# A decoder layer with a routed expert stage: a new order of work in the attention stage, and another way for the expert outputs, the token reads and the stores at the end

## The reference

```
x = x + attn(layernorm(x))            # causal sums of rank 128 (cumsum over tokens), 512 x 512 weights
x = x + xattn(layernorm(x), ctx)      # 16 heads of 32, softmax over the 750 context rows
x = x + ffn(layernorm(x))
# ffn: logits = x @ gate_w.T + gate_b;  probs = softmax over the tokens (axis -2)
#      each of 32 experts takes its 8 best tokens:  vals, idx = top_k(probs, 8)
#      merged[b, e] = sum_k vals * x[idx]                       (one row for each batch and expert)
#      o[b, e] = (gelu([merged, 1] @ w1[e]), 1) @ w2[e]          (513 x 2048, then 2049 x 512)
#      out[b, idx] += vals * o[b, e]                            (scatter back to the 8 tokens)
```

## Time and profile before

| | us |
|---|---|
| median of 3 runs | 2212.28 (2208.69 to 2214.53) |
| the profiled execution's own time | 2212.52 |
| its span | 2210.8 |
| PE busy, of 1290 us from 110 to 1400 us | 1256.5 |
| DMA rate from 1560 to 2100 us | 421 GB/s |

### The profile page before, as it was taken

How to read it: one execution, slowest core, us unless ns; L and a number is a source line. 1 busy time by engine, 2 the same in 40 slices (tenths; PEclk the granted TensorE clock), 3 DMA queues, 4 the chain that set the end, 5 groups by cost and what they waited for, 6 DMA issues and landing times. The chain is left out here.

```text
span 2210.8 us, 41404 instructions
## 1 busy us (share of the span) xinstructions
PE 1842.7 (83%) x12594; PEld 1207.2 (55%) x12594; DVE 1011.4 (46%) x2542; ACT 747.3 (34%) x1551; POOL 823.9 (37%) x591
## 2 busy tenths in 40 slices
PE   7889999999999999999999999986665656655644
PEld 5667777777777776777777767753111111111111
DVE  1355757657667676676676665751100000000003
ACT  3144435435454454454444544542100000000000
POOL 0255545555555556555555565552000000000000
PEclk9799999999999999999999999988877777777776
DMA  5324333243243333332433333266999999999996
GB/s 171 84 68 101 81 91 98 76 101 82 77 105 83 88 94 83 92 85 76 109 83 84 95 85 89 70 240 233 406 422 421 423 421 420 421 422 421 420 365 238
DMA packets 142370, 421.35 MB, mean 191 GB/s; under 512 B 32140, under 2 KB 78188, under 8 KB 117756
## 3 DMA queue, kind: packets, MB, share of 16 engines
q1 hardware_dynamic: 135580, 411.70, 54.6%
q10 hardware_dynamic: 5760, 8.15, 1.0%
q0 software_dynamic: 992, 1.02, 0.1%
HBM read 307.37 MB, written 17.14 MB: 147 GB/s over the span
## 5 line engine op out<-in xcount | busy, mean ns | idle before, releaser
L1172 DVE TENSOR_REDUCE maxes<-bank 112x1 f32<-112x376 f32 (+1 forms) x1024 | 511.3, 539 | 118.5 <-PE bank L1393 114.9
L974 ACT ACTIVATE probs<-bank 125x448 f32<-125x448 f32 x768 | 400.0, 547 | 140.5 <-PE bank L1415 139.5
L1809 PE MATMUL bank<-ring,hid_T 128*32 128x512 f32 x1024 | 177.9, 858 | 201.3 <-DMA ring<-in_L_ffn_w 196.4
L848 POOL TENSOR_TENSOR psum_keys<-psum_keys,probs 125x896 f32<-125x896 f32 x127 | 266.7, 2100 | 211.9 <-ACT probs L974 202.5
L1415 PE MATMUL bank<-q_st,k_st 98*125 98x224 f32 x1536 | 334.6, 304 | 8.5 <-DMA q_st<-max_two 5.6
L1393 PE MATMUL bank<-k_st,q_st 96*112 96x376 f32 (+1 forms) x1024 | 318.9, 357 | 21.3 <-DVE maxes L1172 18.1
L1415 PEld LDWEIGHTS bank<-q_st,k_st 98*125 98x125 f32 x1536 | 256.8, 190 | 61.3 <-issue 33.5
L1713 DVE TENSOR_TENSOR o_fin<-bank,b_row 16x512 f32<-16x512 f32 x32 | 21.7, 678 | 586.6 <-PE bank L1762 586.6
L851 POOL TENSOR_TENSOR psum_keys<-psum_keys,probs 125x896 f32<-125x896 f32 x127 | 266.8, 2100 | 10.0
L1642 POOL DMA_DIRECT2D o_rows<-o_fin x31 | 15.3, 492 | 595.4 <-DVE o_fin L1713 595.4
L1809 PEld LDWEIGHTS bank<-ring,hid_T 128*32 128x32 f32 x1024 | 44.9, 151 | 310.3 <-issue 304.8
(11 more groups left out here) (171 smaller groups left out, 2742.5 us busy)
## 6 DMA issues: line engine op xcount, KB each, us to landing
ring<-in_L_ffn_w SPq DMA_DIRECT2D x128, 2048.0 KB, 30.7
k_st<-k_hi SPq DMA_DIRECT2D x512, 93.8 KB, 2.1
k_st<-k_lo SPq DMA_DIRECT2D x256, 93.8 KB, 2.2
q_st<-q_hi SPq DMA_DIRECT2D x504, 28.0 KB, 1.8
ctx_nat<-in_ctx SPq DMA_DIRECT2D x16, 750.0 KB
x_in<-in_x SPq DMA_DIRECT2D x16, 448.0 KB, 3.9
out<-x SPq DMA_DIRECT2D x16, 448.0 KB, 3.1
out<-ring ACTq DMA_DIRECT2D x28, 256.0 KB, 3.1
```

The costliest lines, as they stand in the source:

```text
L848: nc.gpsimd.tensor_tensor(psum_keys[:], psum_keys[:], lo, ALU.add).then_inc(pool_chain, 1)
L974: nc.scalar.activation(probs[n % 2][:, j, :], bank[5 + u % 2][0:SK, 0:2 * T], ACT.Exp, scale=SCALE).then_inc(probs_ready, 1)
L1172: nc.vector.tensor_reduce(maxes[:, j, t, c:c + 1], score_bank(n)[0:TT, 0:SC[c + 1] - SC[c]], AX.X, ALU.max).then_inc(s_drained, 1)
L1809: last = nc.tensor.matmul(bank[5 + e2][c * 32:(c + 1) * 32, :], hid_T[:, e2, t, c * 32:(c + 1) * 32], ring[:, slot, col:col + D], start=(t ...
```

## The change

1. **A new table.** `TIMETABLE`, `AT`, `MAXIMA` and `SUM_AT` hold other steps, `LAST_PV_AT` is 2 instead of 1. The set of jobs and their sizes stay.
2. **Joined denominators.** `denominators` of a group is issued directly behind the `values` of its last third, instead of later in step 2.
3. **Expert outputs straight into the scatter's operand.** For experts 0 to 30 POOL issues four DMAs each, from `o_fin` into the rows of `o_in` (4 rows of 2 KB each). `o_rows`, the writes to it and the eight reads back are gone. DVE waits for these placements before it writes `o_fin` again.
4. **The last expert by TensorE.** A matmul with a 0/1 matrix `spread` (cleared by POOL, filled by one DVE copy) adds the four partial sums of the last expert and puts them into their rows in one step; DVE adds that to `o_in`, which holds b2 there (four small DMAs at the start of the stage). This is done once for each of the four quarters of `o_in`, the first ahead of the scatter, the others inside it. The last `sum_parts`, the last addition of b2 and the DMAs of L1630 are gone.
5. **The last w2 in another layout.** Its two chunks hold steps t = 0, 1 and t = 2, 3, so that PE starts the first half when the first chunk is there.
6. **The order of SP's queue.** All weights come first, and the token reads behind them. The last two experts are outside PE's loop.
7. **Stores on two queues.** ACT stores the tiles of even number in the order of work, SP those of odd number.

```diff
-LAST_PV_AT = 1
-SUM_AT = {5: 0, 11: 1, 14: 2}
+LAST_PV_AT = 2
+SUM_AT = {6: 0, 12: 1, 13: 2}
...
-MAXIMA = ((3, 3, 3, 1, 2, 2, 0, 0, 0, 1, 1),
-          (0, 1, 0, 0, 0, 3, 1, 3, 1, 2, 1, 2, 2),
-          (1, 2, 1, 0, 2, 2, 0, 2, 2, 0, 1, 1, 2),
-          (4, 0, 1, 0, 1, 2, 1, 1, 0, 2, 1, 2, 1))
+MAXIMA = ((2, 3, 3, 1, 2, 2, 0, 0, 0, 0, 2, 1),
+          (0, 0, 0, 0, 0, 3, 0, 4, 3, 0, 1, 2, 3),
+          (3, 1, 0, 0, 2, 2, 0, 0, 3, 1, 1, 2, 1),
+          (4, 0, 0, 2, 2, 0, 1, 0, 0, 3, 2, 0, 2))
...
                 def last_values(kind, b, kt):
                     if kt:
                         values(b, kt - 1, 2)
+                        denominators(b, kt - 1)
                     elif kind != "first":
                         values(b - 1, G - 1, 2)
+                        denominators(b - 1, G - 1)
...
-                            if s == LATE_AT:
-                                if kt:
-                                    denominators(b, kt - 1)
-                                elif kind != "first":
-                                    denominators(b - 1, G - 1)
...
+        def load_steps(sp, e, q, slot):
+
+            src = w2[e, 0:H1, :].rearrange("(c p t) n -> p c (t n)", p=P, t=HT)
+            n = HT // 2 * D
+            sp.dma_start(ring[:, home_of(slot), :].rearrange("p (c n) -> p c n", c=HC),
+                         src[:, :, (q - 2) * n:(q - 1) * n]).then_inc(chunk_in[slot], 16)
+
+        def place_rows(eng, e, done):
+            for g in range(GB):
+                eng.dma_start(o_in[e:P:E, g, :], o_fin[g * RW:(g + 1) * RW, e % 2, :]
+                              ).then_inc(done, 16)
+
+        def store(eng, n):
+            k = tile_at(n)
+            eng.wait_ge(fin_ready, n + 1)
+            eng.dma_start(rows_out[:, k, :], fin(k)).then_inc(fin_stored[n % 2], 16)
...
-                weights(end, 1, False, (0, 1))
-                def read_back(r, e0, e1):
-                    sp.dma_start(o_in[r * E + e0:r * E + e1, :, :],
-                                 o_rows.rearrange("(g r) e n -> r e g n", r=RW)[r, e0:e1, :, :]
-                                 ).then_inc(o_loaded, 16)
-
-                sp.wait_ge(o_stored, 16 * (E - 4))
-                for r in range(RW):
-                    read_back(r, 0, E // 2)
+                weights(end, 1, False)
                 for g in range(-(-NT // PER)):
                     sp.wait_ge(h_full if g < 2 else o_full, E - 1)
                     n = min(PER, NT - g * PER)
                     sp.dma_start(ring[:, g, 0:n * D].rearrange("p (k d) -> p k d", d=D),
                                  rows_out[:, g * PER:g * PER + n, :]).then_inc(fin_loaded[g], 16)
-                weights(end, 1, False, (2, 3))
-                sp.wait_ge(o_stored, 16 * (E - 1))
-                for r in range(RW):
-                    read_back(r, E // 2, E - 1)
-                sp.wait_ge(o_out, E)
-                for g in range(GB):
-                    sp.dma_start(o_in[E - 1:P:E, g, :], o_fin[g * RW:(g + 1) * RW, 1, :]
-                                 ).then_inc(o_loaded, 16)
+                for n in range(1, NT, 2):
+                    store(sp, n)
...
+                for e in range(E - 1):
+                    pool.wait_ge(o_out, e + 1)
+                    place_rows(pool, e, o_placed)
...
+                def place_last(g):
+
+                    if g == 0:
+                        pe.wait_ge(o_copied, E)
+                        pe.wait_ge(spread_ready, 1)
+                    elif g == 1:
+                        pe.wait_ge(o_out, E - 1)
+                    else:
+                        pe.wait_ge(fin_ready, drained(g * CYCLE - 8))
+                    nc.tensor.matmul(bank[g * CYCLE % 8][:], spread[:, g, :], o_sb[:, 1, :],
+                                     start=True, stop=True).then_inc(last_spread, 1)
```

More of the change, by code:

```diff
@@ L32 @@
 TIMETABLE = (
-    [(0, s, j) for s, j in ((1, "v4"), (2, "v5"), (2, "q3"), (4, "k3.0"), (5, "k3.1"),
-                              (6, "xt0"), (7, "xt1"), (8, "out0"), (9, "ct0"), (11, "out1"),
-                              (11, "ct1"), (13, "pz"), (14, "pc"), (15, "pa"))]
-    + [(1, s, j) for s, j in ((1, "ct2"), (2, "mix0"), (2, "ct3"), (4, "mix1"), (5, "k0.0"),
-                              (8, "yt0"), (9, "yt1"), (11, "q0"))]
-    + [(2, s, j) for s, j in ((0, "k0.1"), (1, "rt0"), (2, "rt1"), (5, "gate"), (10, "q1"),
-                              (12, "wt0"), (12, "wt1"), (13, "merge"))]
-    + [(3, s, j) for s, j in ((0, "k1.0"), (1, "k1.1"), (2, "mt"), (5, "q2"), (7, "v0"),
-                              (9, "v1"), (10, "k2.0"), (11, "k2.1"), (13, "v2"), (14, "v3"))]
+    [(0, s, j) for s, j in ((1, "q3"), (2, "v4"), (3, "v5"), (4, "k3.0"), (5, "k3.1"),
+                              (6, "xt0"), (9, "ct0"), (9, "out0"), (9, "xt1"), (11, "ct1"),
+                              (12, "pz"), (14, "pc"), (15, "pa"), (15, "out1"))]
+    + [(1, s, j) for s, j in ((0, "ct2"), (2, "ct3"), (2, "mix0"), (4, "mix1"), (5, "k0.0"),
+                              (8, "yt0"), (9, "yt1"), (11, "q0"), (15, "rt0"))]
+    + [(2, s, j) for s, j in ((0, "k0.1"), (1, "rt1"), (4, "gate"), (10, "q1"), (11, "wt0"),
+                              (12, "wt1"), (13, "merge"))]
+    + [(3, s, j) for s, j in ((0, "k1.0"), (0, "k1.1"), (4, "mt"), (5, "q2"), (8, "v0"),
+                              (9, "v1"), (10, "k2.0"), (12, "k2.1"), (13, "v2"), (15, "v3"))]
 )
@@ L1517, in build @@
         lay.close()
+        RW = 4
+        GB = B // RW
         hid = sb(es, "hid", [P, 2, BANK])
@@ L1553, in build @@
         fin_ready = sem("fin_ready")
-        fin_stored = sem("fin_stored")
+        fin_stored = [sem(f"fin_stored{i}") for i in range(2)]
         NT = B * T // P
@@ L1586, in weights @@
                             sp.wait_ge(o_full, i * 2 + (e2 - 1))
-                        load_chunk(sp, e, q, slot)
+                        if isinstance(e, int) and e == E - 1 and q >= 2:
+                            load_steps(sp, e, q, slot)
+                        else:
+                            load_chunk(sp, e, q, slot)
                     if 3 not in qs:
+                        return
+                    if isinstance(i, int) and e == E - 1:
                         return
@@ L1602, in _ @@
                                  ).then_inc(picks_loaded, 16)
+                for g in range(GB):
+                    sp.dma_start(o_in[E - 1:P:E, g, :],
+                                 w2[E - 1:E, H1, :].to_broadcast([RW, D])
+                                 ).then_inc(last_bias, 16)
                 weights(1, 0, False, (1, 2, 3))
@@ L1673, in _ @@
                     hidden(i, 1, False)
-                for n in range(NT):
-                    k = tile_at(n)
-                    act.wait_ge(fin_ready, n + 1)
-                    act.dma_start(rows_out[:, k, :], fin(k)).then_inc(fin_stored, 16)
-                act.wait_ge(fin_stored, 16 * NT)
+                for n in range(0, NT, 2):
+                    store(act, n)
+                act.wait_ge(fin_stored[0], 16 * (NT // 2))
             @block.vector
@@ L1734, in _ @@
                     add_biases(i, 1, False)
-                row_out(E // 2 - 1, 1, False)
+                def place_last(g):
+                    dve.wait_ge(last_spread, g + 1)
+                    nc.vector.tensor_tensor(o_in[:, g, :], o_in[:, g, :],
+                                            bank[g * CYCLE % 8][:], ALU.add
+                                            ).then_inc(last_placed, 1)
+                dve.wait_ge(o_placed, 16 * GB * (E - 1))
+                dve.wait_ge(last_bias, 16 * GB)
+                place_last(0)
                 for n in range(NT):
                     k = tile_at(n)
+                    if n % CYCLE == 4 and n // CYCLE + 1 < GB:
+                        place_last(n // CYCLE + 1)
                     dve.wait_ge(fin_loaded[k // PER], 16)
@@ L1801, in expert @@
                         pe.wait_ge(o_copied, e - 1)
-                    for q in (2, 3):
+                    by_step = isinstance(e, int) and e == E - 1
+                    for q in (2,) if by_step else (2, 3):
                         pe.wait_ge(chunk_in[e2 * 4 + q], i * 16 + 16)
                     for t in range(HT):
+                        if by_step and t == 2:
+                            pe.wait_ge(chunk_in[e2 * 4 + 3], i * 16 + 16)
                         for c in range(HC):
-                            slot = home_of(e2 * 4 + 2 + c // 2)
-                            col = (c % 2 * HT + t) * D
+                            slot = home_of(e2 * 4 + 2 + (t if by_step else c) // 2)
+                            col = (c * 2 + t % 2 if by_step else c % 2 * HT + t) * D
                             last = nc.tensor.matmul(bank[5 + e2][c * 32:(c + 1) * 32, :],
```

51 lines of the change are left out of this document (28 added, 23 removed).

## The result

The median went from 2210.49 us (the kernel before, timed with it) to 2181.76 us (runs from 2181.03 to 2182.75): ratio 0.987, 95% interval 0.985 to 0.989. It is faster, as forecast, and inside the range of 2147 to 2187; the likeliest value of 2167 was 15 us too low. The profiled execution took 2181.48 us with a span of 2179.7, so 31.1 us less than the span of 2210.8 before, against 45 forecast.

What follows compares the result with a forecast made beforehand. PE was taken to bound 110 to 1400 us, DMA 1560 to 2100 us. The profiled 2212.5 us less 16 (joined denominators) and 29 (end) gave 2167.5, the median 0.2 lower: 2167 us, range 2147 to 2187.

Steps and rivals of the forecast that it cites:

- Joined denominators, 16 us: Attention stage: joining saves PE 0.27 us of tile switching per group, in 60 groups, 16 us.
- The rest of the table: I let these cancel: Attention stage: the new table's other shifts in waits and switches cancel, taken as zero.
- rival (b): Attention stage: the table also takes most of PE's waits, 16 to 28 us more gained, 2145 us; chance 0.14.
- The wait for POOL: Joined denominators: PE's wait for `psum_keys` is about nil, at most 0.3 us in one group of four, 5 us.
- rival (c): Attention stage: joined denominators wait 0.27 to 0.4 us a group for POOL, gain gone, 2183 to 2191 us; chance 0.12.
- rival (e): Attention stage: a long POOL wait delays ACT and POOL's own next sum, a loop, 2212 to 2224 us; chance 0.04.
- Hidden by the weights: Expert stage: the placements, 32 KB per expert in four POOL DMAs, cost no time beside the weight reads.
- The reads back, 13.4 us: End: dropping the eight `o_rows` reads saves 2.5 us of bytes plus 6.0 and 4.9 us of slow stretches.
- rival (d): End: slowness belongs to token or mixed reads and returns with stores; 11 us not won, 2178 us; chance 0.10.
- The end, 29 us: After the experts: 13.4 us from reads back, 15.1 from closing the idle DMA stretch, some 0.5 from the stores' ramp.
- The forecast's 2146: End: the last w2, no longer behind SP's token issues, lands at about 2146 us.
- Part 7: End: splitting the stores over two queues costs nothing as long as DMA has work; no gain counted.

Runs made afterwards that it cites:

- a_unjoined: Changed kernel with `denominators` back at the end of step 2 on their own, new table kept: 2194.24 us, 0.9927 of the kernel before.
- a_max1: Changed kernel with the old `MAXIMA` row of group 1: 2178.12 us, 0.9856 of the kernel before.
- b_table: Kernel before with the new tables and joined denominators, its expert stage and end unchanged: 2202.27 us, 0.9958 of the kernel before.
- b_joined: Kernel before with joined denominators and its own old tables: 2278.62 us, 1.030 of the kernel before.
- a_place_act: Changed kernel with the placement DMAs issued by ACT instead of POOL: 2187.93 us, 0.9888 of the kernel before.
- b_four_wide: Kernel before with each write to `o_rows` cut into four DMAs of 16 rows and a quarter of the columns: 2210.30 us, 1.000 of the kernel before.
- b_four: Kernel before with each write to `o_rows` in DRAM cut into four DMAs of four rows: 2221.30 us, 1.0041 of the kernel before.
- a_tokens_early: Changed kernel with the last two w2 chunks behind the token reads, as before the change: 2194.29 us, 0.9924 of the kernel before.
- a_one_queue: Changed kernel with all 28 stores on ACT's queue: 2180.64 us, 0.9861 of the kernel before.
- a_rows_once: Changed kernel with one 16-row DMA per expert to `o_rows` and one ACT read back into 128 partitions: 2174.35 us, 0.9834 of the kernel before.

## Why the prediction was right in kind and 15 us too low

**Joined denominators, 16 us: the mechanism and the price hold.** `a_unjoined` puts 0.30 us on a group (0.27 forecast) and the rows show the two steps of 0.78 and 0.49 us; the last 0.03 is that the next operation now follows after 0.49 and not after the 0.52 that was to stay. The Trainium skill's drain (TensorE: Matmul & The Clock Gate, Step-by-step), which would have made 6 us of it, is too small for what leaving the 32-column tiles and entering them again costs here; the measurement decides. Up to the first `o_sb` copy it gave 10.8 us (1546.07 to 1535.26), not 16: the 13 batches between the first and the last but two `gate` jobs give 15.6 (255.01 to 1407.78 in `a_unjoined`, 254.88 to 1392.01 in the changed kernel), and what follows takes 5.0 back (138.3 and 143.3 us to the first copy).

**"The rest of the table: I let these cancel" came out in sum, by luck.** The start of three operations tells the parts of the attention stage apart:

| | first `gate` | 14th `gate` | first `o_sb` copy |
|---|---|---|---|
| kernel before | 256.56 | 1401.93 | 1547.66 |
| new table, not joined (`a_unjoined`) | 255.01 | 1407.78 | 1546.07 |
| changed kernel | 254.88 | 1392.01 | 1535.26 |

The new table by itself moves the first copy by 1.6 us, near the zero that was taken. But over the 13 batches in the middle it costs 7.4 us, 0.57 a batch, and behind them it gains as much. So a batch takes 87.43 instead of 88.05 us, a gain of 0.62 where 1.08 was forecast. PE's waits fell by 11.3 us in all, as rival (b) wanted, and no gain in the period goes with it. `a_max1` shows that the group's `MAXIMA` row is 0.06 of the 0.57. Where the other 0.5 us lie isn't shown: no wait on PE's list accounts for them. The table part as a whole measured 12.4 us instead of 16, and 9.5 by the first copy of `b_table`.

**The wait for POOL, "about nil", holds, and rival (c) did not come.** There is none in the middle batches, with 0.48 us to spare in the group of the earlier trace rows. `b_joined` shows that the concern was real: with the old tables the wait is 1.8 us and the kernel is 3% slower. The 40.6 us of waits are the 3.1 us a batch that its expectation had, but thirteen batches took 1201.3 us instead of 1145.4: 4.3 more a batch, not 2. That fits rival (e)'s loop, a delay that comes round through ACT (PE's waits for it rose from 1.6 to 7.6 us) and POOL, but the loop wasn't followed in the trace. The new table is worth its 0.57 us a batch, because it is what makes the join possible.

**Part 3, "Hidden by the weights": this is the step that failed.** The placements move the same bytes and POOL has all the time for them, but the weights did not hide them. They took 9.7 us from the first to the 31st expert. What was ruled out: the issuing engine (`a_place_act`) and, with DRAM as the target, the number of DMAs, of bytes and of packets (`b_four_wide`). What remains for 6.3 of the 9.6 us up to the 30th copy is that each DMA has four rows (`b_four`). The other 3.3 us are open. The four other kernels with the changed kernel's placements (`a_tokens_early`, `a_max1`, `a_unjoined`, `a_one_queue`) lose 7.1 to 9.0, so a part is chance; and the rate, 415 GB/s with SBUF as the target and 420 with DRAM, speaks for a part of the target.

Why four rows cost anything isn't shown. The Trainium skill (DMA: Bandwidth & Descriptors, Why a DMA increments its semaphore by 16 and not by 1) says that a DMA is spread over the largest number of engines up to 16 that divides its slowest dimension, so four for four rows. That could fit: a 2 MB weight chunk needs all 16 engines and is there when the slowest is done, and the engines that also had a row are late. In `b_four` the bytes come at nearly the full rate while the copies fall behind, as it would be if single engines were late. The same section has DMAs of ACT's queue always take the lowest-numbered engines, so that the same four would be loaded each time, and `a_place_act` was the slowest of all (576.7 us up to the 30th copy). For POOL's queue, however, it has four consecutive engines, taken in turn, so that the four DMAs of an expert would reach all 16, as one DMA of 16 rows does; by that the loss with POOL stays unexplained. The traces don't show which engine carried a packet, so the shape is shown, for DRAM as the target, and the engines are only argued. Nor is it explained why the kernels without this loss have three or four intervals of 18.6 us among those of 20.3, and those with it none or one, at 20.4 to 20.5: half of the loss is in these.

**The reads back, 13.4 us, and rival (d).** The slow stretches are gone and don't return with stores or tokens (396 and 381 GB/s), so (d) falls. `a_rows_once` shows that it was the way of these reads and not their bytes.

**The end, 29 us: measured 28.4.** In detail some errors cancel. The last w2 was ready at 2142.85. The forecast's 2146 is counted from the old start of the 31st expert's w2, 2125.93; from the new one, 2122.48, it is 2142.5, so this holds. From there to the first store went 10.3 us, not 8.2, since the half of w2 behind the last chunk took 3.6 instead of 2.6 us and the matmul with `spread` 2.1 instead of 1.1, both at a granted clock of 0.50 (1.2 GHz). The clock had fallen from 1.00 between 2138.0 and 2138.5, inside the first half of this w2, after PE had waited 1.8 us for the gelu, and from 2156 on it was 1.00 again. So the store came 2.3 us late, and nothing was lost by it, because DMA had tokens to read: its share is 1.04 throughout. The mixed stretch ran at 396 GB/s, above the 383 that was taken; the limit of 358 that the Trainium skill gives (DMA: Bandwidth & Descriptors, Where 436 GB/s comes from) does not show in it.

**Part 7** is worth nothing, as said (`a_one_queue`).

The sum as measured: 2210.8 - 12.4 + 9.7 - 28.4 = 2179.7. Without the failed step it would have been 2170. `a_rows_once`, which has no placements, has a span of 2172.7: its experts take 583.4 us, but its end 53.5 instead of 50.9.

## What to carry to other kernels

When DMA is the bound, a small transfer beside the stream is not free because its bytes are few. Here 16 rows in one DMA, or 16 rows cut by columns into four, cost nothing on their way to DRAM, and four DMAs of four rows did. Measure the stream's period rather than the small DMA, and compare it over stretches that hold nothing else. A stream's slow stretch belongs to a form of transfer until an experiment with the same bytes in another form says otherwise. A table of steps and an edit that reorders work are one change: the join alone cost 3% and with its table it gained, so try an edit together with what makes room for it before giving it up.

## What the runs showed of the hardware

- Four DMAs of four rows (8 KB each) to DRAM beside each expert's 8.4 MB of weights lengthened the time from the first to the 30th expert from 563.6 to 569.9 us; four DMAs of sixteen rows with the same bytes left it at 563.3. With SBUF as the target it was 573.2, and the rate fell from 421 to 415 GB/s.
- While rows were read from DRAM into 15 or 16 partitions at a time, in eight DMAs of SP's queue, the whole stream ran at 200 GB/s; one DMA of ACT's queue with the same 1 MB into 128 partitions ran with it at 386.
- Stores and reads mixed ran at 396 GB/s, no slower than stores alone (383).
- Waits of PE that vanish from the list need not shorten the period: 11.3 us fewer of them went with a batch that was 0.57 us longer before the join was counted, and in `a_max1` 12.7 us more of them with a batch that was no longer.
